# Gate multiplication one iteration later, and the two expert layers alternating by halves on TensorE

## The reference

```python
logits = xf @ Wr + br
topv, _ = lax.top_k(logits, 2)
masked = jnp.where(logits >= topv[:, 1:2], logits, -jnp.inf)
weights = jax.nn.softmax(masked, axis=-1)
h = gelu(einsum('td,edh->eth', xf, W1) + b1, approximate=False)   # H = 1024
expert_out = einsum('eth,ehd->etd', h, W2) + b2
out = einsum('etd,te->td', expert_out, weights)
x = x + tanh(g_ffn[0]) * out
```

## Time and profile before

| what | value |
|---|---|
| median of three runs | 892.22 us |
| the profiled execution's own time | 895.73 us |
| its span, first to last instruction | 893.9 us |
| mean granted TensorE clock, of full speed | 0.956 |
| PE busy | 786.2 us, 88% of the span |
| DVE busy | 582.6 us, 65% |
| ACT busy | 486.0 us, 54% |
| POOL busy | 352.4 us, 39% |

### The profile page before, as it was taken

How to read it: one execution, slowest core, us unless ns; L and a number is a source line. 1 busy time by engine, 2 the same in 40 slices (tenths; PEclk the granted TensorE clock), 3 DMA queues, 4 the chain that set the end, 5 groups by cost and what they waited for, 6 DMA issues and landing times. The chain is left out here.

```text
span 893.9 us, 27595 instructions
## 1 busy us (share of the span) xinstructions
PE 786.2 (88%) x8684; PEld 720.4 (81%) x8685; DVE 582.6 (65%) x1457; ACT 486.0 (54%) x1205; POOL 352.4 (39%) x390
## 2 busy tenths in 40 slices
PE   4499999999999999998539879999999999999993
PEld 3389888898888889898439778888888888888882
DVE  2368999999999988988735345554555555555442
ACT  2156656665555556665225445666555555556652
POOL 2234655555555565546411122222222222222222
PEclk9699999999999999999659999999999999999996
DMA  8875888777778899974366975333334333332212
GB/s 183 147 140 128 162 179 173 137 148 155 162 167 211 196 220 191 191 156 151 132 149 155 271 113 70 52 51 47 49 50 51 47 49 50 51 51 26 25 21 28
DMA packets 124028, 105.84 MB, mean 118 GB/s; under 512 B 60928, under 2 KB 117632, under 8 KB 121728
## 3 DMA queue, kind: packets, MB, share of 16 engines
q1 hardware_dynamic: 110032, 85.51, 46.4%
q0 software_dynamic: 13296, 18.23, 13.0%
q10 hardware_dynamic: 576, 0.56, 0.2%
HBM read 36.54 MB, written 32.19 MB: 77 GB/s over the span
## 5 line engine op out<-in xcount | busy, mean ns | idle before, releaser
L1265 POOL DMA_INDIRECT out_rows<-yg,gates x71 | 114.6, 1614 | 321.1 <-ACT yg L1299 288.0
L1426 PE MATMUL bank<-wts,hh 128*128 x1704 | 203.9, 276 | 24.8 <-DVE hh L1321 21.5
L1290 ACT ACTIVATE hf<-bank,b1t,gscale 128x128 f32<-128x128 f32 x568 | 206.4, 468 | 31.5 <-issue 17.6
L1412 PE MATMUL bank<-xh,wts 128*128 128x128 f16 x3408 | 204.4, 220 | 15.2 <-issue 15.2
L1412 PEld LDWEIGHTS bank<-xh,wts 128*128 x3408 | 198.8, 99 | 16.8 <-issue 15.2
L1426 PEld LDWEIGHTS bank<-wts,hh 128*128 128x128 f16 x1704 | 162.7, 99 | 57.3 <-issue 37.2
L1320 DVE TENSOR_SCALAR hh<-hf,hscale 128x512 f16<-128x512 f32 x142 | 69.1, 486 | 201.6 <-ACT hf L1290 199.9
L1044 PE MATMUL bank<-va,probs 128*128 128x102 f32 x1024 | 139.7, 278 | 9.0 <-DVE ao L740 9.0
L540 POOL TENSOR_SCALAR_AFFINE_SELECT xh<-rowmax 128x512 bf16<-128x512 bf16 x128 | 94.2, 736 | 135.7 <-DVE rowmax L792 127.5
L1044 PEld LDWEIGHTS bank<-va,probs 128*128 128x128 f32 x1024 | 126.3, 193 | 12.2 <-DVE ao L740 6.8
L1299 ACT ACTIVATE yg<-yb,gates 128x256 f32<-128x256 f32 x71 | 36.1, 508 | 157.3 <-DVE yb L1331 140.7
(11 more groups left out here) (169 smaller groups left out, 975.6 us busy)
## 6 DMA issues: line engine op xcount, KB each, us to landing
wts<-in_W SPq DMA_DIRECT2D x16, 1024.0 KB, 7.1
wts<-keys SPq DMA_DIRECT2D x96, 128.0 KB
wts<-queries SPq DMA_DIRECT2D x96, 128.0 KB, 5.5
split_weights<-wts SPq DMA_DIRECT2D x8, 1024.0 KB, 5.1
wts<-split_weights SPq DMA_DIRECT2D x8, 1024.0 KB, 7.4
xin<-in_x SPq DMA_DIRECT2D x16, 256.0 KB, 2.7
cin<-in_ctx_in SPq DMA_DIRECT2D x16, 256.0 KB, 3.1
out_rows<-x SPq DMA_DIRECT2D x16, 256.0 KB, 4.4
```

The lines of the kernel that those rows point to most:

```text
L1265: pool.indirect_dma_start(out=out[:, :], out_offset=bass.IndirectOffsetOnAxis(ap=numbers, axis=0), in_=yg[m % 2][:, :], in_offset=None, co ...
L1290: last = act.activation(hf[b][:, c, :], HB[2 * b + half][:, c % 4 * TILE:(c % 4 + 1) * TILE], ACT.Gelu, bias=b1t[:, bass.ds(e, 1), c], sca ...
L1412: last = pe.matmul(HB[2 * b + half][:, c % 4 * TILE:(c % 4 + 1) * TILE], weight(expert[1], first_at(wp, k, c), P), xh[(m + 1) % RING][:, x ...
L1426: last = pe.matmul(YB[b][:, 0:D], hh[b][:, hp, c, :], weight(expert[0], second_at(wp, c), D), start=q == 0, stop=q == 23)
```

## The change

On ACT the gate multiplication stands one iteration later: iteration i is now Gelu of tile i+1, then `yg` of tile i-1, which waits for the scatter of tile i-3. One more iteration is run at the end for the last `yg`. On PE iteration i is now written as: first half of the first layer of tile i+1, first half of the second layer of tile i, second half of the first layer of tile i+1, second half of the second layer of tile i. The register work goes from the whole second layer into its second half, but for `expert_in_turn`, which comes behind matmul 8 of the first half.

```diff
-            peeled(first + RING * rounds, hi)
+            peeled(first + RING * rounds, hi + 1)
...
-                    if there(0):
-
-                        e = expert_of(act, i)
-                        act.wait_ge(yb_ready, i + 1)
-                        when(act, before(i, 2), added, added_value(i - 2))
-                        act.activation(yg[m % 2][:, :], yb[m % 2][:, :], ACT.Copy,
-                                       scale=gates[m][:, bass.ds(e, 1)]).then_inc(yg_ready, 1)
+                    if there(-1):
+
+                        e, p = expert_of(act, i - 1), (m - 1) % 2
+                        act.wait_ge(yb_ready, i)
+                        when(act, before(i, 3), added, added_value(i - 3))
+                        act.activation(yg[p][:, :], yb[p][:, :], ACT.Copy,
+                                       scale=gates[(m - 1) % RING][:, bass.ds(e, 1)]).then_inc(yg_ready, 1)
...
-                        for c in range(HC):
-                            half = c // 4
-
-                            when(pe, c % 4 == 0 and before(i + 1, 2), gelu_ready, (i - 1) * 2 + half + 1)
...
-                        terms = [(hp, wp, c) for half in range(2) for hp, wp in ((0, 0), (1, 0), (0, 1))
-                                 for c in range(4 * half, 4 * half + 4)]
-                        for q, (hp, wp, c) in enumerate(terms):
-                            if q % 12 == 0:
-                                pe.wait_ge(split_ready, i * 2 + q // 12 + 1)
...
-                                if q == 2:
-                                    following = expert_in_turn(i + 2)
-                                if q in (5, 7, 9, 11, 13, 15):
-                                    lo = (q - 5) * 3
-                                    addresses(following, first[lo:lo + 6], 2 * (P - 1))
-                                if q in (19, 21):
-                                    lo = (q - 19) * 3
-                                    addresses(expert[1], second[lo:lo + 6], 0)
+                    for half in range(2):
+                        if there(1):
+                            b = (m + 1) % 2
+                            terms = [(wp, xp, k) for wp, xp in ((0, 0), (0, 1), (1, 0)) for k in range(KC)]
+                            when(pe, before(i + 1, 2), gelu_ready, (i - 1) * 2 + half + 1)
+                            for c in range(4 * half, 4 * half + 4):
+                                for q, (wp, xp, k) in enumerate(terms):
...
+                            last.then_inc(h_psum, 1)
+                        if there(0):
+                            b = m % 2
+                            if half == 0:
+                                when(pe, before(i, 2), yb_ready, i - 1)
+                            pe.wait_ge(split_ready, i * 2 + half + 1)
+                            terms = [(hp, wp, c) for hp, wp in ((0, 0), (1, 0), (0, 1))
+                                     for c in range(4 * half, 4 * half + 4)]
...
+                                if main and i + 2 < MAIN_TILES and there(2):
+                                    if half == 0 and q == 8:
+                                        following = expert_in_turn(i + 2)
+                                    if half == 1 and q < 8:
+                                        if q < 6:
+                                            addresses(following, first[6 * q:6 * q + 6], 2 * (P - 1))
+                                        else:
+                                            addresses(expert[1], second[6 * q - 36:6 * q - 30], 0)
                     if there(0):
...
                         last.then_inc(y_psum, 1)
```

More of the change, by code:

```diff
@@ L1417, in it @@
-                    if there(0):
-                        b = m % 2
-                        when(pe, before(i, 2), yb_ready, i - 1)
-                        terms = [(hp, wp, c) for half in range(2) for hp, wp in ((0, 0), (1, 0), (0, 1))
-                                 for c in range(4 * half, 4 * half + 4)]
-                        for q, (hp, wp, c) in enumerate(terms):
-                            if q % 12 == 0:
-                                pe.wait_ge(split_ready, i * 2 + q // 12 + 1)
-                            last = pe.matmul(YB[b][:, 0:D], hh[b][:, hp, c, :],
-                                             weight(expert[0], second_at(wp, c), D), start=q == 0, stop=q == 23)
-                            if main and i + 2 < MAIN_TILES and there(2):
-                                if q == 2:
-                                    following = expert_in_turn(i + 2)
-                                if q in (5, 7, 9, 11, 13, 15):
-                                    lo = (q - 5) * 3
-                                    addresses(following, first[lo:lo + 6], 2 * (P - 1))
-                                if q in (19, 21):
-                                    lo = (q - 19) * 3
-                                    addresses(expert[1], second[lo:lo + 6], 0)
@@ new lines, in it @@
+                    for half in range(2):
[5 more added lines that the diff above has]
+                                for q, (wp, xp, k) in enumerate(terms):
+                                    last = pe.matmul(HB[2 * b + half][:, c % 4 * TILE:(c % 4 + 1) * TILE],
+                                                     weight(expert[1], first_at(wp, k, c), P), xh[(m + 1) % RING][:, xp, k, :],
+                                                     start=q == 0, stop=q == 5)
+                            last.then_inc(h_psum, 1)
[6 more added lines that the diff above has]
+                                     for c in range(4 * half, 4 * half + 4)]
+                            for q, (hp, wp, c) in enumerate(terms):
+                                last = pe.matmul(YB[b][:, 0:D], hh[b][:, hp, c, :],
+                                                 weight(expert[0], second_at(wp, c), D),
+                                                 start=half == 0 and q == 0, stop=half == 1 and q == 11)
+                                if main and i + 2 < MAIN_TILES and there(2):
[6 more added lines that the diff above has]
+                                            addresses(expert[1], second[6 * q - 36:6 * q - 30], 0)
```

## The result

The changed kernel takes 867.85 us (median of four runs, 865.51 to 871.22), against 891.93 us for the kernel before in the same comparison. The ratio is 0.9737, with a 95% interval from 0.9698 to 0.9777: faster by 2.6%. The forecast was 864.6 us, with a range from 856 to 880.

What follows compares the result with a forecast made beforehand. The prediction took the Gelu, hh, yb, yg chain through ACT and DVE as the bound, with PE following. Gains of 22.9 (steady) and 5 (opening) less 0.3 (end) make 27.6 us, from 892.2 to 864.6 us; range 856 to 880.

Steps and rivals of the forecast that it cites:

- The circle: On ACT and DVE: chain Gelu, hh, yb, yg, next Gelu sets the tile, 5.68 us between Gelus; the change opens it.
- The steady tile at 5.30 us: Tiles 14 to 70: PE's own pace, 5.30 us a tile, replaces 5.731; 22.9 us gained.
- the group load: PE's sequencer: a load of 0.33 us for every fourth tile, charged at 0.02 us a tile, 1.2 us in all.
- The rival in which PE's busy time can't be compressed: Steady stretch: recorded PE busy time is real, a tile takes 5.48 us, total 873.5 us; chance 0.13.
- The halves: PE's two layers by halves: still 5.30 us a tile, with 2.5 us of latency to spare.
- The register work: PE's sequencer, beside 1.31 us of matmuls instead of 2.62: cost taken as 0, bounds 0 to 0.75 us a tile.
- The sequencer rival: PE's register work not covered by the sequencer's lead: 0.75 us more a tile, 905.5 us in total; chance 0.06.
- The opening: Eight tiles from 493.96 to 548.01: Gelu waits for a scatter landing one tile older; 5 us gained, bounds 0 to 11.6.
- The hand replay: Opening replayed with the profile's durations: tile 11's first layer starts near 526 in place of 531.5.
- The clock: PE in the opening: two stretches at lower granted clock after idling, about 1.6 us lost each, inside the 5 us.
- The rival with the low clock: PE's clock low for each tile's second layer: 6.9 us a tile, some 953 us in total; chance 0.02.
- The end: After tile 69's second layer: last scatter starts 11.2 us later instead of 10.9, the scatter chain being late; cost 0.3 us.

Runs made afterwards that it cites:

- `yb` first: Kernel before with one DVE edit: in iteration i, yb of tile i comes before hh of tile i+1; 863.45 us, ratio 0.971.
- `yg`-between run: Changed kernel with four yg buffers and the gate multiplication of tile i-1 between the two halves of tile i+1's Gelu; 855.15 us, ratio 0.963.

## Why the prediction was right, point by point

- **The circle.** Right, and shown from three sides: moving the gate multiplication alone gives the whole gain, changing PE's order alone gives none, and breaking the circle at another link gives nearly all of it too (5.327 us a tile).
- **The steady tile at 5.30 us.** Right: 5.300. The whole saving there is 24.1 us between the two first profiles, 23.4 from the second profile of before. I had taken off 1.2 us for the group load; it costs nothing. The rival in which PE's busy time can't be compressed (5.48 us) is refuted: 306.95 us of "busy" became 296.80 for the same matmuls.
- **The halves.** I had costed them at nothing, right for the steady stretch. I had not seen that they can cost something where PE must wait anyway, as in the opening.
- **The register work.** Right at 0: with all of it beside 1.31 us of matmuls the 5.300 us do not move, nor do they when it is spread. The 0.75 us are the sum of the durations only: in the tile above the sequencer starts these instructions, which have matmuls between them, over some 1.8 us, from 604.84 to 606.60. That is more than the 1.31 us of matmuls, and the first starts 0.93 us ahead of them (605.77), so the lead that the forecast counted on is there and is used. The sequencer rival (905 us) is refuted. The Trainium skill (TensorE: Matmul & The Clock Gate, the table at its head) gives PE's queue a depth of 64 instructions, which is room for such a lead; no run here measured the depth.
- **The opening.** The hand replay was good: it put tile 11's first layer near 526, 32.0 us after tile 6's, and the first profile after has 32.0 (495.46 to 527.50, before 37.6). The reason that I gave, waits for an older landing, is not shown. In the first pair of profiles ACT's waits for scatters fell from 16.6 to 10.4 us, but they are five in place of three, not one fewer, and in the second pair they are 12.9 and 12.7 us. `yb` first leaves every Gelu behind the same landing as before and has as short an opening (47.54 us), and the gate multiplication alone has 47.97 us with as much as 20.3 us of such waits. What these kernels share is the open circle, which then most likely gives much of the gain; how much stays open. The size was off too. I took 5 us from one profile in which the opening lasted 54.05 us, which makes 49.05 after; the profiles have 48.02 and 48.44, but the second one before has 50.19. The gain is 6.0 us in the first pair, 1.8 in the second, 3.9 on average.
- **The clock.** I expected two stretches of lower clock in the opening. There was one in the first profile after (the second layer at 521.89 took 2.24 us for 12 matmuls, where 1.47 is usual), none in the second, and none in the steady stretch. The rival with the low clock is refuted.
- **The end.** Right: the last scatter starts 11.3 us after the end of tile 69's second layer (844.27 + 1.31 = 845.58), forecast 11.2, before 10.9. The scatters, not PE, set it, as the `yg`-between run shows. The forecast steps of 4.66 us were 4.5 and 5.1. From tile 70's first layer on, the end takes 25.09 and 25.08 us after, 24.97 and 25.23 before: no cost that two profiles can tell.
- **The total.** 27.6 us forecast; 24.1 between the medians, 20 to 27 by the interval, so the forecast is somewhat too high. The saving was read from one execution, 3.5 us slower than the median, and then taken off the median. Between the two first profiled executions it is 28.6 us (895.73 to 867.12), near the forecast; between the second ones it is 24.2 (890.07 to 865.87), near the medians. On average of the two pairs the steady stretch gave 23.8 us (forecast 22.9), the opening 3.9 (5) and the end 0.0 (-0.3), together 27.7. That this meets the 27.6 is partly luck: the group load, which costs nothing, and the opening were missed by about 1 us in opposite directions. Against it stands the start of the stage, 1.6 us later on average in the profiles after. It lies in code that the change doesn't touch and scatters by 7 us between profiles, so I take it for noise.

Here are the opening's rows of the profile after, which answer to the earlier trace rows.

```profile
509.47 0.51 ACT L1299 ACTIVATE yg<-yb,gates 128x256 f32<-128x256 f32 x1 [2.83 <-DMA out_rows<-yg,gates]
...
518.10 0.51 ACT L1299 ACTIVATE yg<-yb,gates 128x256 f32<-128x256 f32 x1 [4.97 <-DMA out_rows<-yg,gates]
518.69 1.53 POOL L1265 DMA_INDIRECT out_rows<-yg,gates  x1 [7.09 <-ACT yg L1299]
521.89 2.24 PE L1426 MATMUL bank<-wts,hh 128*128 x12 [3.16 <-DVE hh L1321]
523.41 0.51 ACT L1299 ACTIVATE yg<-yb,gates 128x256 f32<-128x256 f32 x1 [1.67 <-DMA out_rows<-yg,gates]
```

The wait at 499.19 is gone and the next two are shorter, and three more of 1.67 us and less follow; but the landing near 518 is where it was, since the scatters are no quicker.

## What to carry to other kernels

When two helper engines take turns in program order, look for a circle in which an old tile's last step stands in front of a new tile's first step on both of them; moving one of the two steps past the other tile's opens it, and which one hardly matters for the pace (5.300 and 5.327 us a tile here). A busy share near 90% on a pipelined engine is no proof that it is the bound: read its pace from a stretch in which it waits for nobody. A step moved later can eat a gain at the end of the program, where a serial chain behind it starts later: PE's idle before the last tile went from 3.00 to 0.46 us and the end got no shorter. A finer place for the step (between the halves) made the end 3 us shorter.

## What the runs showed of the hardware

- PE's distance between starts was the same in every kernel that let it run free: 296.80 us for 56 tiles in six kernels and seven profiles, 55.8 ns for a 128-column and 109.2 ns for a 256-column matmul with its weight load. The Trainium skill (TensorE: Matmul & The Clock Gate, "Back-to-back issue gap") gives a sustained 81 ns for the former. The trace disagrees: in the steady stretch of the first profile after, no two first-layer matmuls in a row start more than 57 ns apart within a half.
- Changing the layer, and with it the PSUM bank and what is stationary, four times a tile instead of twice cost 0: 296.80 us for 56 tiles with the halves and without them.
- An idle time of 2.92 us in front of a second layer left the granted clock at 1.00 (24 matmuls in 2.78 us, above), while 1.15 us in the first profile of before was followed by the lower one (4.13 us for 21), and so was 2.85 us in the second profile of the halves alone (507.44, 2.66 us for 12). The length of the last idle time alone doesn't tell whether the clock falls.
- A scatter of 128 rows lands in 3.9 us in the median of the first profile of before and in 9.1 us at most; the five issued from 480 to 522 have a median of 8.5 us, and SyncE loads the last experts' weights then (issues from 480.85 to 507.69).
